# A convolution kernel with group normalisation: eight rows of the last image loaded by GpSimd's queue, on fourteen of sixteen DMA engines

## What is computed

```python
def reference(x, weight, bias):
    ...
    g = x.reshape(8, 16, 2, 128, 128)
    g = (g - mean(g)) / sqrt(var(g) + 1e-5)
    fx = fft2(pad(g, 256), norm='ortho')
    wf = fft2(pad(weight, 256), norm='ortho')
    sp = ifft2(einsum('bihw,oihw->bohw', fx, wf), norm='ortho').real
    return x + sp[:, :, 64:192, 64:192] + bias
```

## Time and profile before

| what | value |
|---|---|
| median of 3 runs | 83.18 us (83.04 to 83.39) |
| the profiled execution, its own time | 83.37 us |
| span of it, from first to last instruction | 82.1 us |
| TensorE busy | 67.9 us, 83% |
| VectorE, ScalarE, GpSimd busy | 50.2, 47.9, 30.2 us |
| HBM read and written | 16.84 MB and 16.78 MB, 409 GB/s |
| packets of SyncE's queue | 2160, 33.56 MB |

### The profile page before, as it was taken

The page is one execution under the profiler, slowest core; times in us unless marked ns, Lnnn a source line. Parts: engine busy times, 40 slices in busy tenths (PEclk is TensorE's granted clock), DMA queues, the critical chain, the costliest instruction groups (busy, mean ns, idle before and its releaser), DMA issues.

```text
span 82.1 us, 682 instructions
## 1 busy us (share of the span) xinstructions
PE 67.9 (83%) x222; PEld 41.9 (51%) x222; DVE 50.2 (61%) x43; ACT 47.9 (58%) x53; POOL 30.2 (37%) x41
## 2 busy tenths in 40 slices
PE   0009865999999999999999999999999999998000
PEld 0015424656666666666666666566666665664000
DVE  0019937950399779949985995899499626001600
ACT  4307958980299669938965994798399561000000
POOL 6994000000039940000997590095039107600000
PEclk9999996556999999999999999999999999999955
DMA  1999999999988998999796997999889999999992
GB/s 23 319 427 475 431 399 455 431 423 447 543 383 383 511 415 381 441 441 454 311 590 287 511 511 335 431 495 415 367 383 471 415 415 455 407 423 401 429 419 123
DMA packets 2209, 33.62 MB, mean 409 GB/s; under 512 B 257, under 2 KB 289, under 8 KB 545
## 3 DMA queue, kind: packets, MB, share of 16 engines
q1 hardware_dynamic: 2160, 33.56, 96.2%
q10 hardware_dynamic: 48, 0.06, 0.4%
HBM read 16.84 MB, written 16.78 MB: 409 GB/s over the span
## 4 chain that ended last, share of the span: by engine, by line
PE 76%; DMA 14%; DVE 2%; SPq 1%; issue 0%; POOL 0%; POOLq 0%
PE ps L413 74%; DMA x<-x_dram 14%; DVE x L429 2%; PE ps_m L319 1%; SPq L182 1%; PE ps_w L266 1%; POOL pair L214 0%; POOL eps L186 0%; POOLq L568 0%
## 5 line engine op out<-in xcount | busy, mean ns | idle before, releaser
L413 PE MATMUL ps<-g,w_sb 128*128 128x363 f32 (+1 forms) x192 | 62.0, 480 | 0.0
L413 PEld LDWEIGHTS ps<-g,w_sb 128*128 128x128 f32 x192 | 36.7, 197 | 20.6 <-issue 2.6
L284 DVE TENSOR_REDUCE sums<-x 128x1 f32<-128x4096 f32 x7 | 30.9, 4410 | 0.6 <-DMA x<-x_dram 0.6
L395 POOL TENSOR_SCALAR x<-x,bias_sb 128x1984 f32<-128x1984 f32 (+3 forms) x12 | 23.2, 1947 | 21.2 <-ACT origin L293 16.0
L304 ACT ACTIVATE unused<-x,origin 128x4096 f32<-128x4096 f32 (+1 forms) x9 | 30.0, 3330 | 0.3
L429 DVE SCALAR_TENSOR_TENSOR x<-ps,bias_sb,x 128x1089 f32<-128x1089 f32 (+2 forms) x9 | 10.9, 1220 | 7.7 <-PE ps L413 7.7
L374 ACT ACTIVATE g<-x,rstd 128x1089 f32<-128x1089 f32 (+2 forms) x8 | 9.4, 1188 | 3.4 <-DVE rstd L348 3.4
L284 DVE TENSOR_REDUCE first_sums<-x 128x1 f32<-128x2048 f32 x2 | 4.6, 2286 | 6.0 <-DMA x<-x_dram 6.0
L259 POOL COPY sums<-x 128x1 f32<-128x1 f32 x6 | 1.0, 187 | 18.7 <-DMA x<-x_dram 18.7
L336 DVE TENSOR_SCALAR var<-ps_m,square 128x1 f32<-128x1 f32 x8 | 1.7, 218 | 9.5 <-ACT square L331 9.5
L331 ACT ACTIVATE square<-ps_m,origin 128x1 f32<-128x1 f32 x8 | 2.1, 261 | 8.6 <-PE ps_m L319 8.6
(11 more groups left out here) (19 smaller groups left out, 11.6 us busy)
## 6 DMA issues: line engine op xcount, KB each, us to landing
out_dram<-x SPq DMA_DIRECT2D x2, 4096.0 KB, 11.8
x<-x_dram SPq DMA_DIRECT2D x3, 2048.0 KB, 15.3
out_dram<-x SPq DMA_DIRECT2D x3, 2048.0 KB, 7.5
x<-x_dram SPq DMA_DIRECT2D x1, 4096.0 KB, 28.9
x<-x_dram SPq DMA_DIRECT2D x1, 3328.0 KB, 36.3
x<-x_dram SPq DMA_DIRECT2D x2, 1024.0 KB, 5.9
out_dram<-x SPq DMA_DIRECT2D x1, 1056.0 KB, 4.8
out_dram<-x SPq DMA_DIRECT2D x1, 992.0 KB, 9.4
```

Source lines behind the costliest of these rows:

```text
L284: lambda e: e.tensor_reduce(to_sum(img, k)[:, 0:1], piece, mybir.AxisListType.X, ALU.add),
L395: put("pool", lambda e: e.tensor_scalar(part, part, 1.0, bias_sb, op0=ALU.mult, op1=ALU.add), *free, mark=mark)
L413: lambda e, k=k, dc=dc, rows=rows, top=top: e.matmul(ps[:, 0:rows, 0 : N - dc], w_sb[:, k * P : (k + 1) * P], g[:, top : top + rows, dc:N] ...
```

## The change

The last pair's load is cut anew. `begin` ends eight rows earlier (`SHARE`), and these eight rows of image 7 are loaded for partitions 0 to 125 (`MOST`) by a transfer that GpSimd's queue issues, behind the first `take_first` in its order. Its source is read in three parts in turn, (b a) n -> a b n, so that the outermost size is 42 on one side and 126 on the other; the host lays these rows of x out in the matching order. Partitions 126 and 127 of the rows stay with SyncE, as a transfer of its own whose semaphore the last load shares. A tiny transfer of 6 x 2 x 2 numbers (`turn`) goes ahead of GpSimd's. Both of GpSimd's transfers count on one semaphore, `moved`, whose state GpSimd resets (`dma_reset`) in the turn of image 3, after it has waited for it. The waits of image 7's rows change to fit.

```diff
+    SHARE = 8
+    MOST = 126
...
-    whole, begun = pairs[3].rearrange("p b h w -> p (b h w)"), (2 * H - LAST) * W
-    source = x[3].rearrange("p b h w -> p (b h w)")
+    whole, source = (p.rearrange("p b h w -> p (b h w)") for p in (pairs[3], x[3]))
+    end, begun = (2 * H - LAST) * W, (2 * H - LAST - SHARE) * W
     begin = load(whole[:, :begun], source[:, :begun])
-    loaded[6] = [(H, begin)]
-    loaded[7] = [(H - LAST, begin), (H, load(whole[:, begun:], source[:, begun:]))]
+    tail = load(whole[MOST:P, begun:end], source[MOST:P, begun:end])
+    tail = load(whole[:, end:], source[:, end:], shared=tail[1])
+
+    put.semaphore("moved")
+
+    def spread_load(to, of):
+        return put("pool", lambda e: e.dma_start(to, of), adds="moved")
...
+    turn = sbuf("turn", 6, 2, 4)[:, :, 0:2]
...
     normalize(0)
     take_first(2, w_ok)
 
+
+    spread_load(turn, wb[0:6, 0 : 2 * C].rearrange("p (a b) -> p a b", a=2)[:, :, 0:2])
+    share = spread_load(whole[0:MOST, begun:end], source[0:MOST, begun:end].rearrange("(b a) n -> a b n", b=3))
+    loaded[6] = [(H, begin)]
+    loaded[7] = [(H - LAST - SHARE, begin), (H - LAST, share), (H, tail)]
...
             if img == B - 5:
+                number = put.sems["moved"].num
+                put("pool", lambda e: e.dma_reset(range(number, number + 1)), share)
                 take_first(img + 4)
...
+    part = arrays["x_dram"][-1, :126, 1, 32:40]
+    part[:] = part.reshape(42, 3, *part.shape[1:]).transpose(1, 0, 2, 3).reshape(part.shape)
```

More of the change, by code:

```diff
@@ L177, in conv_preact_kernel, with load @@
     loaded = {}
-    def load(to, of, *needs, by="sp"):
-        name = f"load{len(put.sems)}"
-        put.semaphore(name)
+    def load(to, of, *needs, by="sp", shared=None):
+        name = shared or f"load{len(put.sems)}"
+        if not shared:
+            put.semaphore(name)
         return put(by, lambda e: e.dma_start(to, of), *needs, adds=name)
```

## The result

The changed kernel takes 83.80 us (median of 11 runs, 83.61 to 84.22), the kernel before 83.39 us beside it (median of 11, 83.04 to 83.56): a ratio of 1.006, 95% interval 1.004 to 1.008. It is slower by 0.41 us, about half a per cent, and lies 0.2 us above the upper end of the range that was given. Of the 0.62 us between 83.80 and the 83.18 on which the sums were put, the other 0.21 are the kernel before itself, whose median was 83.18 of three runs then and is 83.39 of eleven here. The profiled execution took 83.67 us, with a span of 82.4 us (82.1 before).

The account below looks back on a forecast made before the run. Full DMA engines (96.2% of span) bound it, the last to finish its stores setting the end. Of 0.60 us removed and 0.80 added on fourteen engines, a term of -0.05 was taken: 83.18 - 0.05 = 83.1 us, range 82.5 to 83.6.

Parts of the forecast that it names:

- Added: GpSimd's new load: nine 2 KB packets on each of fourteen engines, 0.80 us, so 0.20 us more net (upper end 0.94).
- Removed: SyncE's load `begin`: eight packets per engine shrink from 26 to 24 KB, 0.60 us less on each of sixteen engines.
- Price of a packet: DMA queues in full flow: 0.0373 us a KB plus 0.014 fixed, so 0.089 us for 2 KB; upper end 0.171.
- The second rival: New load's 2 KB packets cost 0.171 us: 84.1 us, 13%; signs: packets above 0.11 us, first store issued after 41.0 us.
- The wait behind it: First store waits for `begin` on every engine: issue moves from 40.63 to 40.83 us, store packets from 41.50 to about 41.70.
- The late engine: End of the stores: one unidentified DMA engine draws packets alone after fifteen others finish, costing some 0.6 to 0.9 us.
- the case that it is left out: Slowest engine among the two without new rows: keeps 0.08 us; otherwise 0.20 us later. Taken: -0.05 us.
- SyncE, GpSimd, the loads behind: Extra issues, GpSimd's reset and images 3 to 5 landing up to 0.80 us later on fourteen engines: no cost expected.
- The rule against the change: Skill's rule that spreading DMAs over issuing engines does not help bandwidth, all sharing sixteen engines: sum 0, time 83.2 us.
- The first rival: At the stores' end, the slowest engine is left out and keeps all 0.60 us saved: 82.6 us, 27%.
- The third rival: GpSimd's 126 rows are dealt to all sixteen engines, 0.11 us more on each: 83.3 us, 10%.

Follow-up runs that it names:

- own rows: Changed kernel with GpSimd's queue loading the eight rows for all 128 partitions over sixteen engines, each writing its usual rows; 83.44 us, ratio 1.000.
- two transfers: Changed kernel with GpSimd's queue loading the eight rows for all 128 partitions as two transfers of four rows each; 83.26 us, ratio 1.000.
- ScalarE's two runs: Changed kernel with the rows issued by ScalarE, no tiny transfer or reset: 126 rows on fourteen engines, 84.24 us; all 128 partitions on sixteen, 83.60 us.
- the crossed run: Changed kernel with GpSimd's queue loading the eight rows as two transfers of 64 partitions, each over all sixteen engines; 84.67 us, ratio 1.013.
- The run with 40 rows: Changed kernel with 40 rows instead of 24 in the last load (`LAST = 40`), so the first store is issued earlier; 83.53 us, ratio 1.004.

## Why the prediction was wrong

A gain of 0.05 us was forecast, as good as no change, and the kernel is half a per cent slower. The step that failed is the one headed *Added*, with that headed *Removed*: both price only the packets that an engine gains or loses, and put at nothing what the new packets do to the ordinary ones beside them.

- **Price of a packet:** right. 2 KB cost 0.08 us against 0.089 forecast, though GpSimd's rows mostly travel two to a packet (the 0.12 MB of 26 to 30 us make 29 packets of 4 KB). As packets of 2 KB, from ScalarE's queue, they cost 0.107 x 3.5 x 16 / 68 = 0.088 us. The second rival, dear small packets, gave 84.1 us and one of its two signs, a first store after 41.0 us; its mechanism is not what happened.
- **Added: "fourteen engines have 0.20 us more".** The nine rows cost what was said, but the sum left out that the packets already in the queue would stretch. At 1.366 us for 1.215, five or six packets of 32 KB on an engine lose 0.75 to 0.9 us during the transfer. With 0.72 (nine rows at 0.08) and less 0.60 that is 0.9 to 1.0 us, an estimate, against the 0.80 by which the first store was late; 0.20 was forecast. With own rows from the same queue the sum comes out nearly as I had made it: eight rows on each engine give 0.11 us, and the first store was 0.03 us late, or 0.22 with two transfers.
- **Removed: "two have 0.60 us less".** This counts bytes by the engine that carries them. By the chains the two engines left out lose 8 x (1.31 - 1.214) = 0.77 us in pair 2, as much as the others, so that they end their loads a little later than before and not 0.60 us earlier. The dealing of rows made 0.6 us between ScalarE's two runs (84.24 and 83.60) and 1.2 us between the crossed run and that with own rows (84.67 and 83.44), each pair with the further differences named above. Under the port theory the engines left out still have their rows written beside them, in the way of their own packets. That the resource is the port is inferred: the mapping in the Trainium skill ("SBUF — State Buffer", section "Door 1: The DMA port swizzle") is consistent with it, but no run here looks into a port.
- **The wait behind it:** right as a mechanism. The store packets started from 42.20 us, 0.8 us behind the issue as before, and engines stood idle ahead of it (share 0.85). Its price was set by the late landing, not by the 0.20 us of the sum. The run with 40 rows shows what it may be worth: some 0.3 us between the medians, 83.80 and 83.53, with intervals that overlap.
- **The late engine:** the case that it is left out was the one taken, and it holds; since no row told which case it would be, that is luck. In the profiled executions the others' end moved by 0.7 us or more and the span by 0.3: the lag shrank by about half a microsecond and paid for part of the loss. That is a start ahead of the rest, 42.29 us against 42.44 to 42.74 on the fourteen, and not the saved 0.60 us. With another pair left out nothing pays, and the loss by the medians is about 0.8 us (84.14 against 83.34 without the tiny transfer, 84.24 against 83.38 from ScalarE's queue, 84.08 against 83.26 from SyncE's).
- **SyncE, GpSimd, the loads behind:** right. GpSimd's timeline, beside the earlier trace rows:

```profile
18.73 0.77 POOL L206 DMA_DIRECT2D turn<-wb_dram  x1 [0.47 <-issue]
19.50 0.67 POOL L206 DMA_DIRECT2D x<-x_dram  x1
22.90 0.18 POOL L268 COPY sums<-x 128x1 f32<-128x1 f32 x1 [2.74 <-DMA x<-x_dram]
23.90 5.54 POOL L404 TENSOR_SCALAR x<-x,bias_sb 128x3968 f32<-128x3968 f32 x2 [0.82 <-issue]
...
45.84 3.03 POOL L404 TENSOR_SCALAR x<-x,bias_sb 128x1984 f32<-128x1984 f32 x2 [1.16 <-ACT origin L302]
```

The two issues take 0.77 and 0.67 us and end well before the copy, which still waits 2.74 us for its load; the reset leaves 1.16 us of idle time ahead of the bias step.

- **The rule against the change:** no queue of the three gained anything. With that agrees the rule of the Trainium skill ("DMA: Bandwidth & Descriptors", section "Rules for kernel authors") that spreading DMAs over issuing engines does not help bandwidth; the loss of 0.41 us it does not give.

The first rival (all saved bytes kept) needed a transfer that leaves two engines free; in these runs every way of giving their rows to other engines cost more than it freed. The third rival (dealt to all sixteen) did not happen: two chains have no row of the new load.

## What to carry to other kernels

Where DMA engines are full, bytes per engine need not be the whole of their work: here rows dealt to other engines than usual stretched the ordinary packets on every engine, also on those that carried none of the rows. To even out DMA engines by moving rows between them, first time the move beside a full queue with the same bytes dealt the usual way; the difference is what the dealing costs. And where a later step waits for a load on all engines, relief of some engines is worth nothing until the slowest of them is earlier too.

## What the runs showed of the hardware that I had not expected

- A transfer of 0.26 MB, 0.8% of the traffic, slowed the ordinary packets beside it by 12% (1.215 to 1.366 us for 32 KB) when its rows were dealt to fourteen engines, and by 2% (1.214 to 1.236 us) when an ordinary load of all 128 partitions brought them. The two engines that carried none of the rows were slowed as much as the rest (1.31 us in the mean of pair 2).
- One engine ends the stores one to three packets behind the rest in every kernel that did not leave it out. Its lag grows during the stores, since all engines begin them within 0.55 us. It is made packet by packet: in the two traces of the kernel before, the 32 KB packets of its chain take 1.25 us in the mean, those of the other chains 1.22 at most. Why was not found.
- A second queue beside a full one, issued from GpSimd, cost no measurable time as long as rows stayed with their engines (ratio 1.000, interval 0.998 to 1.002).
